# One 8-block attention-and-feed-forward kernel on one core: halved down tiles in the last group, split first products, and a new order on every engine

## The reference

```python
x = x + wkv(time_decay, time_first, layernorm(x), ctx)       # x: (16, 128, 256), scan over 128 steps
#   e1*aa + e2*vt over e1*bb + e2, with running exponent pp, decay w = -exp(time_decay), u = time_first
x = x + ffn(layernorm(x), gate_w, up_w, down_w, gate_s, up_s, down_s)
#   g = einsum('th,ih->ti', xf, gate_w) * gate_s ; u = einsum('th,ih->ti', xf, up_w) * up_s
#   out = einsum('ti,hi->th', silu(g) * u, down_w) * down_s      # 256 -> 704 -> 256 channels
```

## Time and profile before

| | us |
|---|---|
| median of 3 runs (lowest, highest) | 106.54 (106.52, 106.72) |
| profiled execution | 105.73 |
| its span | 103.8 |
| PE busy | 91.5 (88%) |
| DVE busy | 77.0 (74%) |
| ACT busy | 77.4 (75%) |
| POOL busy | 68.0 (65%) |

### The profile page before, as it was taken

The page is one execution under the profiler, slowest core; times in us unless marked ns, Lnnn a source line. Parts: engine busy times, 40 slices in busy tenths (PEclk is TensorE's granted clock), DMA queues, the critical chain, the costliest instruction groups (busy, mean ns, idle before and its releaser), DMA issues.

```text
span 103.8 us, 1619 instructions
## 1 busy us (share of the span) xinstructions
PE 91.5 (88%) x484; PEld 75.0 (72%) x484; DVE 77.0 (74%) x121; ACT 77.4 (75%) x136; POOL 68.0 (65%) x97
## 2 busy tenths in 40 slices
PE   3999888929399999999999999999999999999800
PEld 3968878919298778777787888886877788888500
DVE  1587999999977898999999999996716222945230
ACT  4367999999954999999999999999577426465000
POOL 2029679969997994894898899645399504576000
PEclk9999999999958999999999999999999999999975
DMA  1999999998000000000014000005000000050050
GB/s 31 311 331 403 363 400 373 374 385 321 11 3 3 0 0 6 0 0 0 0 50 152 0 0 6 0 0 202 0 0 0 0 0 3 27 185 0 6 202 6
DMA packets 6475, 10.78 MB, mean 104 GB/s; under 512 B 576, under 2 KB 3648, under 8 KB 6336
## 3 DMA queue, kind: packets, MB, share of 16 engines
q1 hardware_dynamic: 6320, 10.62, 28.8%
q10 hardware_dynamic: 144, 0.03, 0.2%
HBM read 8.55 MB, written 2.10 MB: 102 GB/s over the span
## 4 chain that ended last, share of the span: by engine, by line
PE 64%; DVE 20%; issue 5%; ACT 4%; DVEq 1%; POOL 1%; POOLq 0%; ACTq 0%
PE ps_f L691 35%; PE ps_d L708 17%; DVE sbe L516 5%; DVE sbp L527 5%; PE ps_f L719 4%; DVE den L541 3%; PE ps_x L647 3%; DVE num L551 2%; ACT L348 2%; DVE xl L567 2%; PE ps_a L628 2%; PE ps_x L668 2%; DVEq L58 1%; PE ps_x L653 1%; PE ps_d L653 1%
## 5 line engine op out<-in xcount | busy, mean ns | idle before, releaser
L691 PE MATMUL ps_f<-xh,wgu_r 128*128 128x512 f32 (+1 forms) x94 | 30.3, 404 | 2.2 <-issue 2.0
L334 POOL TENSOR_TENSOR hl<-h,hh 128x512 fp32r<-128x512 f32 x20 | 25.7, 1295 | 8.7 <-ACT hh L450 8.5
L691 PE MATMUL ps_f<-xl,wgu_r 128*128 128x512 f32 (+1 forms) x94 | 29.0, 391 | 1.8 <-DVE xl L567 1.8
L582 DVE SCALAR_TENSOR_TENSOR h<-ps_f,vec,sil 128x512 f32<-128x512 f32 x20 | 14.9, 747 | 11.0 <-PE ps_f L691 5.6
L691 PEld LDWEIGHTS ps_f<-xl,wgu_r 128*128 128x128 f32 x94 | 17.8, 196 | 5.9 <-DVE xl L567 2.3
L691 PEld LDWEIGHTS ps_f<-xh,wgu_r 128*128 128x128 f32 x94 | 17.0, 198 | 6.0 <-issue 2.2
L439 ACT ACTIVATE sil<-ps_f,vec 128x512 f32<-128x512 f32 x20 | 13.6, 686 | 5.5 <-PE ps_f L691 5.3
L708 PE MATMUL ps_d<-hh,wd_r 128*128 128x512 f32 x40 | 16.3, 407 | 0.0
L708 PE MATMUL ps_d<-hl,wd_r 128*128 128x512 f32 x40 | 15.7, 393 | 0.0
L450 ACT ACTIVATE hh<-h 128x512 fp32r<-128x512 f32 x20 | 12.4, 625 | 3.5 <-DVE h L582 3.5
L719 PE MATMUL ps_f<-ident 128*128 128x128 f32 x78 | 11.2, 303 | 1.6 <-POOL ident L247 1.6
(11 more groups left out here) (78 smaller groups left out, 136.7 us busy)
## 6 DMA issues: line engine op xcount, KB each, us to landing
xt<-x_tok SPq DMA_DIRECT2D x8, 256.0 KB, 6.9
xc<-x_ch SPq DMA_DIRECT2D x4, 512.0 KB, 11.0
out_ch<-xc SPq DMA_DIRECT2D x8, 256.0 KB, 2.4
wgu<-w_gu SPq DMA_DIRECT2D x1, 1408.0 KB, 8.4
vc<-v_ch SPq DMA_DIRECT2D x2, 512.0 KB, 10.8
wd<-w_d SPq DMA_DIRECT2D x1, 768.0 KB, 10.7
vt<-v_tok SPq DMA_DIRECT2D x2, 256.0 KB, 5.3
vt<-v_tok SPq DMA_DIRECT2D x1, 512.0 KB, 9.6
```

The lines of the kernel that those rows point to most:

```text
L334: nc.gpsimd.tensor_tensor(hl[:, m, :], h[:, n % HS, :], hh[:, m, :].bitcast(F32), ALU.subtract).then_inc(s_hl, 1)
L582: nc.vector.scalar_tensor_tensor(h[:, n % HS, :] if m < FULL else up, up, vec[r, V_US + m:V_US + m + 1], sil[r, n % 2, :], ALU.mult, ALU.m ...
L691: last = nc.tensor.matmul(ps_f[:, i % RING, ts], w, a, start=c == 0 and x is xh, stop=c == CC - 1 and x is xl)
```

## The change

- The list of calls of every engine is written anew, and the order of the loads.
- The second unit's products of slots 0 to 2 can be issued as two pieces: gateh, uph (high part) and gatel, upl (low part). HALVED goes.
- fill(k), k unread 128-column products into ps_d, is added and called once, with k = 1; the calls of warm have other counts (33 in all, 39 before).
- TAIL is 18: all six down products of the last group are split by chunk. Chunk 1 of the last block also waits (semaphore s_pace) for chunk 1 of block 21.

```diff
-HALVED = 3
-TAIL = 3 * MC + 2
+TAIL = 3 * MC
-            def product(n, part, exact, half=None):
+            def product(n, part, exact, half=None, levels=(0, 1)):
-                if half == 0 or m == 0:
-                    pe.wait_ge(s_xh, units)
+                check = half is not None or m == 0 or g == 0
...
-                for x in (xh, xl):
-                    if x is xl and (half == 0 or m == 0):
-                        pe.wait_ge(s_xl, units)
+                for k in levels:
+                    x = (xh, xl)[k]
+                    if check:
+                        pe.wait_ge((s_xh, s_xl)[k], units)
...
+                if n == GROUPS * MC - 1 and 1 in chunks:
+                    pe.wait_ge(s_pace, 1)
...
+                    elif n == GROUPS * MC - 3 and c == 1:
+                        last.then_inc(s_pace, 1)
...
+            def fill(k):
+
+                for _ in range(k):
+                    nc.tensor.matmul(ps_d[:, 1, 0:P], ident[:, :], ident[:, :], start=True, stop=True)
...
+                def gateh(n):
+                    product(n, 0, exact, 1, (0,))
...
-                up(22); gate(23); down(18); down(19); down(20); downb(20); down(21); downb(21); down(22); downb(22)
-                down(23); downb(23)
+                gate(20); up(20); gate(21); up(21); gate(22); up(22); gate(23); downb(18); downb(19); down(18)
+                downb(20); down(19); down(20); downb(21); down(21); down(22); down(23); downb(22); downb(23)
...
-            load_x(0); load_x(1); load_x(2); load_x(3); load_v(0); load_v(1); load_wgu(); load_x(4); load_v(2)
+            load_x(0); load_x(1); load_x(2); load_x(3); load_v(0); load_v(1); load_wgu(); load_v(2); load_x(4)
```

More of the change, by code:

```diff
@@ L452, in high_h @@
                     nc.scalar.activation(hx[REST:P, :], ps_f[REST:P, slot(n, 1) % RING, :], ACT.Copy).then_inc(s_hh, 1)
[L454 to L462, removed]
@@ L463, in _ @@
-            high_h(14); norm2(7); silu(16); silu(17); high_n(7); high_h(15); high_h(16); high_h(17); silu(18)
-            high_h(18); silu(19); silu(20); high_h(19); silu(21); high_h(20); silu(22); high_h(21); silu(23)
+            rstd1(0); rstd1(1); expk(0); expk(1); elift_(); rstd1(3); expk(2); log_den(0); expk(3); recip(0)
+            wcheck(0); log_den(1); wcheck(1); recip(1); rstd2a(0); wcheck(2); norm2(0); log_den(2); rstd1(5)
+            high_n(0); rstd2a(1); recip(2); expk(4); norm2(1); expk(5); log_den(3); high_n(1); recip(3); tables(SILU)
@@ new lines, in _ @@
+            silu(0); silu(1); high_h(0); norm2(2); silu(2); high_h(1); silu(3); high_h(2); high_n(2); high_h(3)
+            silu(4); silu(5); tables(LN_EXP); log_den(4); rstd1(7); norm2(3); recip(4); high_h(4); high_n(3)
+            high_h(5); expk(6); log_den(5); expk(7); recip(5); tables(SILU); silu(6); norm2(4); silu(7); high_n(4)
+            high_h(6); high_h(7); silu(8); silu(9); tables(LN_EXP); log_den(6); high_h(8); norm2(5); recip(6)
+            high_h(9); high_n(5); tables(SILU); silu(10); silu(11); high_h(10); high_h(11); silu(12); tables(LN_EXP)
@@ L465, in _ @@
+            log_den(7); recip(7); tables(SILU); silu(13); norm2(6); high_h(12); silu(14); high_h(13); high_n(6)
+            silu(15); high_h(14); high_h(15); silu(16); norm2(7); high_h(16); high_n(7); silu(17); high_h(17)
+            silu(18); silu(19); high_h(18); high_h(19); silu(20); high_h(20); silu(21); silu(22); high_h(21); silu(23)
             high_h(22); high_h(23)
@@ L745, in downb @@
                     down_(n, exact, (1,))
[L747 to L750, removed]
@@ L751, in rest_of_program @@
-                gate(12); x1_T(6); up(12); down(9); down(10); down(11); gate(13); up(13); n_T(6); gate(14); up(14)
-                gate(15); x1_T(7); up(15); up(16); gate(16); gate(17); n_T(7); down(12); down(13); gate(18); down(14)
-                down(15); gate(19); up(18); up(19); down(16); gate(20); down(17); up(20); gate(21); up(21); gate(22)
-                up(22); gate(23); down(18); down(19); down(20); downb(20); down(21); downb(21); down(22); downb(22)
-                down(23); downb(23)
+                p_T(3); gatea(0); gatea(1); n_T(1); e_T(4); upa(0); fill(1); uph(0); gateh(0); x1_T(2); gatel(0)
@@ new lines, in rest_of_program @@
+                upl(0); gateh(1); gatel(1); up(1); gate(2); up(2); gate(3); up(3); n_T(2); gate(4); gate(5); x1_T(3)
+                up(4); e_T(5); down(0); down(1); down(2); n_T(3); down(3); up(6); e_T(6); x1_T(4); gate(6); down(4)
+                gate(7); down(5); up(7); n_T(4); gate(8); e_T(7); gate(9); x1_T(5); up(8); down(6); up(9); gate(10)
+                up(10); n_T(5); gate(11); down(7); down(8); x1_T(6); gate(12); up(12); down(9); down(10); gate(13)
+                down(11); gate(14); up(13); up(14); n_T(6); gate(15); up(15); gate(16); x1_T(7); up(16); down(12)
@@ L757, in _ @@
+                down(13); gate(17); n_T(7); down(14); down(15); up(18); gate(18); down(16); gate(19); up(19); down(17)
+                gate(20); up(20); gate(21); up(21); gate(22); up(22); gate(23); downb(18); downb(19); down(18)
+                downb(20); down(19); down(20); downb(21); down(21); down(22); down(23); downb(22); downb(23)
             pe.wait_ge(s_ident, 1)
-            warm(10); x_T(0); x_T(1); warm(3); e_T(0); warm(7); p_T(0); e_T(1); warm(10); p_T(1); e_T(2); y_T(0)
-            warm(1); p_T(2); warm(8); y_T(1); e_T(3); count(); n_T(0)
+            warm(8); x_T(0); warm(8); e_T(0); warm(5); p_T(0); e_T(1); x_T(1); warm(5); p_T(1); e_T(2); y_T(0)
@@ L760, in _ @@
+            warm(2); p_T(2); warm(5); y_T(1); count(); e_T(3); n_T(0)
             pe.wait_ge(s_wgu, 16)
```

51 lines of the change are left out of this document (29 added, 22 removed).

## The result

| us | before | after |
|---|---|---|
| median (lowest, highest), 4 runs each | 106.53 (105.94, 106.72) | 102.60 (102.35, 103.31) |
| profiled execution (its span) | 105.73 (103.8) | 102.64 (100.9) |
| mean granted clock of the profiled execution | 0.966 | 1.00 |

A forecast was written before the change was run, and what follows sets the result against it. Bound by the vector engines up to low_n(1), then PE, first at half clock, then two last residuals with stores. Gains 1.45 + 0.15 + 0 + 0.45 = 2.05 off the median 106.54 gave 104.5 us, range 103.4 to 106.3.

The forecast's parts named there:

- Term 6: End: reordered last down products let residual 0 start earlier; gain 0.45 us, bounds 0.2 and 0.5; stores shift along.
- Terms 1 to 3: Start up to gate(2): earlier low_n(1), products moved into the pause and no clock fall; together 1.45 us gained.
- term 3: PE's clock: with the pause before low_n(1) filled, no fall at 28.5; half clock had cost 1.7 us.
- term 2: Pause before low_n(1): uph(0) and x1_T(2) moved into it, value 0.6 us, 0.4 turned into a wait for silu(0).
- term 1: Start up to low_n(1): first scan some 0.3 us earlier, low_n(1) ends at 28.2 instead of 28.28; gain 0.1.
- Term 4: Stretch from 31 to 93 us: same products, small new waits against removed ones; net gain 0.15 us.
- Term 5: Loads: same bytes in another order, no late arrival; 0 us, at most 0.5 lost.
- a second pause with a fall: Rival: around up(6), PE waits long for low_n(3) or expk(6) and the clock falls; 108.0 us, chance 0.12.
- The clock falls all the same: Rival: the clock still falls at 28.5 despite the filled pause; gain 0.9, 105.6 us, chance 0.20.

The follow-up runs named there:

- e7: Kernel before with only the wait on s_pace added, old order of down products: median 104.70 us against 106.46 for before on that chip.
- e8: The changed kernel run once more, unaltered, on a second chip: median 103.24 us against 106.46 for the kernel before.
- e4: Kernel before with seven unread products filling the pause between gate(0)'s high and low product of unit 1: median 105.14 us against 106.14.
- e3: Kernel before with gateh(0), uph(0) and x1_T(2) put ahead of gatel(0) and upl(0): median 104.88 us against 106.14.
- e12: Kernel before with the last group's down products in the new order (TAIL 18), without s_pace: median 104.65 us against 106.53.
- e5: Changed kernel with the second unit's three products unsplit and without fill(1): median 103.15 us against 103.24 for the changed kernel.
- e2: Changed kernel with the old order and split of the last group's down products, without s_pace: median 104.96 us against 106.14 for before.
- e6: Changed kernel without the wait on s_pace and its increment: median 103.37 us against 103.24 for the changed kernel.
- e9: Changed kernel with the old calls of warm, x_T, e_T and p_T ahead of the branch: median 103.04 us against 106.53 for before.
- e11: Kernel before with a wait at s_pace's place on a semaphore already up, holding nothing: median 105.97 us against 106.53.
- e1: Kernel before with only the new end (all six last down products split, new order, s_pace): median 104.51 us against 106.14.

## Why the prediction was wrong in size and right in sign

**Term 6, the end, is the step that failed.** It said "The stores shift along", without a reason, and put s_pace at 0 because PE loses nothing by it. The residuals' part held: forecast 0.45, measured 1.49 - 1.04 = 0.45. But the store had a wait of its own in it, 1.4 us in the profile, 1.8 in e7's median. It stood in the profile before: 4.3 us from the last residual to the end of the span, while the median store lands in 2.4 (rows 8 give the residual's end, the page's DMA issues the 2.4). I took the store as a constant and never subtracted the two. With 1.4 added, 2.05 becomes 3.45, between e8's 3.2 and the first median's 3.9.

**Terms 1 to 3, the start and the clock: 1.45 forecast, 0.89 in the profile.** Of the mechanism only the clock (term 3) held; term 2 didn't. The clock didn't fall at 28.5. gate(2) came at 31.67 instead of 31.1, and the 0.57 lie in term 1: low_n(1) ended at 28.67, not at 28.2. It is the first scan, forecast 0.3 earlier, that started at 8.94 instead of 8.45. In the changed kernel's execution PE still ran the two matmuls at 5.16 at half clock, 0.73 each, where before those at 5.35 took 0.51. When the clock first rises varies from execution to execution, in these fourteen from 4.4 to 7.7 us, and the first scan goes with it, 8.35 to 9.92. At the same rise (6.0 and 6.1) the changed kernel's first scan starts 0.2 ahead of e4's, which has the old prelude (9.14); so the prelude did nearly what was forecast, and chance took 0.7. The forecast's own prices give 0.2 as well: 16 calls of warm stand ahead of e_T(0) instead of 13, and 0.86 less three times 0.22 is 0.2. silu(0) freed up(1)'s slot near 30.6 rather than 30.1, the same shift.

Term 2 gave the products moved into the pause 0.6, less 0.4 for the wait for silu(0); by the table above they are worth nothing, since at a whole clock gate(2) starts 22.6 us behind the first scan in the old order and 22.7 in the new. The forecast compared the new order with the one profile in which the clock had fallen, and so counted the clock and the order together. Over many runs e3 and e4 put term 3 at 1.0 to 1.3. And "it fell right behind the pause" is no more than where it fell: e12 has the same pause of 1.80 without a fall.

**What the gain is made of.** From profile to profile the span is 2.9 shorter: the first scan is 0.5 later, the way from it to the last gate product 1.54 shorter (the clock), the end up to the last residual 0.44, and the store 1.41. The runs agree. Without a fall among the products before takes 104.5 (10 runs) and the changed kernel 102.6 (7 of its 15), 2.0 less, which is the end's 0.44 and 1.41 and the prelude's 0.2. With one fall it is 106.4 (58 runs) against 103.4 (six at 0.983), 3.0 less.

**The spread of the kernel before was misread.** Three runs within 0.20 "speaks for a fall that comes each time", I wrote, and set the Trainium skill's rule on luck aside. 78 runs show 103.7 to 109.4. The Trainium skill, TensorE: Matmul & The Clock Gate, section "Part 1: The HAM clock gate", says that the place of the transition differs from run to run, and these runs agree; what it gives for the cost of the ramp, under 1% of a typical span, is less than here, where the first rise moved the first scan by up to 1.57 us of some 104. The later falls, which set the three sets of before 2% apart, come on top. It cost the forecast little, since the fall does come in seven of eight executions of before.

**Term 4: 0.15 forecast, 0.15 measured** (0.89 at gate(2), 1.04 at the last gate product; at a whole clock, against e12, too: 59.70 from gate(2) on instead of 59.85). The wait of up(6) for low_n(3), forecast at 0.2, is the 0.21 at 44.68; that for expk(6) didn't come; nor did one at 70, where before had 0.17. **Term 5:** 0, no wait for a load past the branch. add_y(2) ended at 28.69 instead of the 28.2 forecast, so x1_T(2) at 28.75 and low_n(1) came together: the cover of term 2 was as thin as said, and to take the split back (e5) costs nothing.

**The rivals.** The slower one, a second pause with a fall, didn't come: PE has no wait over 0.21 past 31. "The clock falls all the same" came true in about half of the executions, but, in the five profiles of this start that show it (e2, e5, e6, e8, e9), at 23.9 to 24.9, ahead of the place that matters. The range ended at 103.4 because no case in it allowed for anything behind the last residual.

## What to carry to other kernels

Subtract the last store's issue from the end of the span and compare with the median store: a difference is a cost of its own, and one wait or another order in TensorE's last products can remove it. Ask what a filled pause does to the clock, and place it ahead of where the clock would fall. Three equal times are no proof that a clock behaves the same each time: here it took ten to thirty runs to see the sets. Compare executions with the same clock before you credit an order of instructions, for here the new order by itself was worth nothing. Size an edit of the start by executions whose clock rose at the same time, since the rise alone moved the first scan by up to 1.5 us.

## What the runs showed of the hardware

- The fetches of instructions of queue q8 are DMAs of 16 KB, six in an execution, that take 0.9 to 1.5 us each. In six of fourteen profiles packets of 2 KB of the last store (eight in five, one in e11) started when one ended, on one of the 16 DMA engines, 0.7 to 1.3 us after all the others were done, and the store landed after 4.0 to 4.5 us instead of 2.5.
- A wait of TensorE that costs nothing (s_pace) took 1.8 us off the median of a kernel (e7, 104.70 against 106.46), and the same instruction on a semaphore long up took off nothing that these runs can tell (e11, 105.97 against 106.53).
- The same program has executions with no fall of the clock among the products, one and two: 103.7 to 104.7, 105 to 107 and 108 to 109.4 us for the kernel before. A fall at 28.5 to 30.3, where TensorE is what the others wait for, cost 1.5 us up to the last gate product (before, e1, e7, e11 against e12); one at 23.9 to 24.9 in the new start 0.1 to 0.7 (e2, e5, e6, e8, e9 against the changed kernel), but 1.4 in the old order of e3, at 24.7.
- TensorE's clock can stay up through a pause of 1.80 us (e12) behind which it fell in another execution of the same instructions (before).
